# The attention output stored as two bf16 halves and loaded turned by transposing transfers

## The reference

```
x = x + xattn(layernorm(x), ctx, ctx, length)       # q, k with rope; softmax; 16 heads x 64
    out = softmax(q k^T / 8, masked) v              # [2048, 1024]
    return out @ Wo + bo                            # [2048, 256]
x = x + ffn(layernorm(x))                           # 8 experts, FF = 512, top 2 by a gate
```

## Time and profile before

| | before |
|---|---|
| runs, median (lowest to highest) | 1209.41 us (1206.67 to 1213.72) |
| span of the profiled execution | 1211.3 us |
| its mean granted clock of TensorE | 0.965 |
| PE, DVE, ACT, POOL busy | 1070.4, 979.4, 731.4, 644.6 us |
| last store issued, first load of the projection issued | 899.78, 906.04 us |
| first expert tile fetched | 1004.43 us |

### The profile page before, as it was taken

How to read it: one execution, slowest core, us unless ns; L and a number is a source line. 1 busy time by engine, 2 the same in 40 slices (tenths; PEclk the granted TensorE clock), 3 DMA queues, 4 the chain that set the end, 5 groups by cost and what they waited for, 6 DMA issues and landing times. The chain is left out here.

```text
span 1211.3 us, 32849 instructions
## 1 busy us (share of the span) xinstructions
PE 1070.4 (88%) x12843; PEld 709.2 (59%) x13030; DVE 979.4 (81%) x1769; ACT 731.4 (60%) x1298; POOL 644.6 (53%) x457
## 2 busy tenths in 40 slices
PE   1468999999999999999999999999969958999995
PEld 1334566566656656656665665666648944566663
DVE  5878999999999999999999999999944674455552
ACT  2635666666666666666666666766644643455552
POOL 1045764674585477467448647733449554333333
PEclk9679999999999999999999999999988979999998
DMA  8034242332423324143242433317526522333330
GB/s 280 0 97 115 79 107 63 98 91 69 107 79 97 96 81 104 51 122 84 77 99 76 110 79 90 79 38 224 207 99 231 174 84 84 57 52 57 54 60 12
DMA packets 104445, 117.01 MB, mean 97 GB/s; under 512 B 47389, under 2 KB 86494, under 8 KB 103006
## 3 DMA queue, kind: packets, MB, share of 16 engines
q1 hardware_dynamic: 91214, 99.74, 29.5%
q0 software_dynamic: 7152, 8.43, 4.2%
q10 hardware_dynamic: 5920, 6.65, 2.0%
HBM read 39.46 MB, written 36.87 MB: 63 GB/s over the span
## 5 line engine op out<-in xcount | busy, mean ns | idle before, releaser
L829 ACT ACTIVATE prob<-sc,key_bias 128x512 f32<-128x512 f32 x640 | 405.3, 684 | 149.2 <-PE sc L683 145.1
L962 DVE TENSOR_REDUCE part_max<-mx 128x1 f32<-128x427 f32 x768 | 417.3, 590 | 35.8 <-PE mx L700 35.8
L1106 POOL TENSOR_TENSOR prob_lo<-prob 128x1024 bf16<-128x1024 f32 x128 | 242.5, 1894 | 229.4 <-ACT prob L829 229.3
L974 DVE TENSOR_TENSOR prob_lo<-prob 128x1024 bf16<-128x1024 f32 x192 | 278.2, 1449 | 9.8 <-ACT prob L829 6.2
L727 PE MATMUL pv<-VV,prob 128*128 128x65 bf16 x2560 | 267.9, 193 | 3.7 <-POOL prob_lo L1106 3.5
L729 PE MATMUL pv<-VV,prob_lo 128*128 128x65 bf16 x2560 | 269.3, 195 | 0.0
L728 PE MATMUL pv<-VV,prob 128*128 128x64 bf16 x2560 | 268.0, 193 | 0.0
L727 PEld LDWEIGHTS pv<-VV,prob 128*128 128x128 bf16 x2560 | 239.8, 99 | 38.8 <-POOL prob_lo L1106 7.3
L728 PEld LDWEIGHTS pv<-VV,prob 128*128 128x128 bf16 x2560 | 237.2, 97 | 26.4
L683 PE MATMUL sc<-Q,K 65*128 65x512 bf16 x640 | 243.6, 381 | 10.3 <-issue 4.0
L700 PE MATMUL mx<-K,Q 128*128 128x427 bf16 x768 | 236.6, 349 | 9.7 <-DVE part_max L962 5.1
(11 more groups left out here) (208 smaller groups left out, 1470.8 us busy)
## 6 DMA issues: line engine op xcount, KB each, us to landing
expert_inputs<-zeros SPq DMA_DIRECT2D x129, 129.0 KB, 2.8
we<-in_w_exp SPq DMA_DIRECT2D x8, 1536.0 KB, 7.9
Q<-we SPq DMA_DIRECT2D x45, 256.0 KB, 3.8
attention_out<-o_out SPq DMA_DIRECT2D x64, 128.0 KB, 2.0
o_in<-attention_out SPq DMA_DIRECT2D x16, 512.0 KB, 3.7
q32s<-q SPq DMA_DIRECT2D x122, 64.0 KB, 2.0
K<-we SPq DMA_DIRECT2D x48, 160.0 KB, 3.9
VV<-next_v SPq DMA_DIRECT2D x16, 322.5 KB, 4.0
```

The costliest lines, as they stand in the source:

```text
L829: act.activation(prob[:, s % PRING, j, :], sc[n % 2][:], ACT.Exp, bias=key_bias[:, t:t + 1], scale=HD ** -0.5).then_inc(exp_done, 1)
L962: dve.tensor_reduce(part_max[:, b_ % 2, qt, h:h + 1], mx[:, pl.part_banks(qt, h)[0]:pl.part_banks(qt, h)[-1] + 1, 0:pl.width], mybir.AxisL ...
L974: dve.tensor_tensor(prob_lo[:, s % PRING, 0:g, :], prob[:, s % PRING, 0:g, :], hi_half(prob[:, s % PRING, 0:g, :])[:, :, 1::2], ALU.subtra ...
L1106: pool.tensor_tensor(prob_lo[:, s % PRING, 0:g, :], prob[:, s % PRING, 0:g, :], hi_half(prob[:, s % PRING, 0:g, :])[:, :, 1::2], ALU.subtr ...
```

## The change

The DRAM tensor `attention_out` becomes bf16 and twice as wide: for each head pair 128 columns of high halves and then 128 of low halves. `output` on POOL multiplies as before, then casts the result to bf16 (the high half) and subtracts that from the f32 value (the low half); each of the three instructions waits for the one before it by a semaphore. `store` waits for the low half and issues two DMAs of 64 KB in place of one of 128 KB. In the projection SP loads a tile, 128 rows x 2048 columns bf16, again 512 KB, with a transposing DMA into `oT`, where each run of 128 columns arrives turned. The transposes on PE and both splits, `OH` on ACT and `OL` on DVE, are gone, and the matmuls read `oT`. A buffer of `oT` is free when its projection has ended; a buffer of `o_in` was free when its transposes had ended.

```diff
-    o_dram = nc.dram_tensor("attention_out", [S, H * HD], F32, kind="Internal").ap()
+    o_dram = nc.dram_tensor("attention_out", [S, 2 * H * HD], BF16, kind="Internal").ap()
...
+        o_halves = sb("o_halves", [P, 2, 2, QT, HD], BF16)
...
                     def output(p, i):
 
                         need(pool, rden_made, p, BLOCKS, i + 1)
-                        need(pool, o_stored[i % 2], p, 16 * BLOCKS // 2, 16 * (i // 2 + 1))
+                        need(pool, o_stored[i % 2], p, 32 * BLOCKS // 2, 32 * (i // 2 + 1))
                         pool.tensor_tensor(o_out[:, i % 2, :, :], o_raw[:, i % 2, :, 0:HD], rden[:, i % 2, :].unsqueeze(2).to_broadcast([P, QT, HD]),
                                            ALU.mult).then_inc(o_made, 1)
+                        need(pool, o_made, p, BLOCKS, i + 1 + 2)
+                        pool.tensor_copy(o_halves[:, i % 2, 0, :, :], o_out[:, i % 2, :, :]).then_inc(o_hi_made, 1)
+                        need(pool, o_hi_made, p, BLOCKS, i + 1)
+                        pool.tensor_tensor(o_halves[:, i % 2, 1, :, :], o_out[:, i % 2, :, :], o_halves[:, i % 2, 0, :, :],
+                                           ALU.subtract).then_inc(o_lo_made, 1)
...
                     def store(p, i):
                         a, c = set_of(i)
-                        need(sp, o_made, p, BLOCKS, i + 1 + 2)
+                        need(sp, o_lo_made, p, BLOCKS, i + 1)
                         rows = o_dram[c * QC:(c + 1) * QC, :].rearrange("(t p) d -> p t d", p=P)
-                        sp.dma_start(rows[:, :, bass.ds(p * P + a * HD, HD)], o_out[:, i % 2, :, :]).then_inc(o_stored[i % 2], 16)
+                        for z in range(2):
+                            sp.dma_start(rows[:, :, bass.ds((2 * p + z) * P + a * HD, HD)], o_halves[:, i % 2, z, :, :]).then_inc(o_stored[i % 2], 16)
...
-        o_in = sb("o_in", [P, OB, J * P])
-        OH = sb("OH", [P, 2, J, P], BF16)
-        OL = sb("OL", [P, 2, J, P], BF16)
+        oT = sb("oT", [P, OB, 2 * J, P], BF16)
...
                 for t in range(ST):
                     if t >= OB:
-                        sp.wait_ge(ot_ready, t - OB + 1)
-                    sp.dma_start(o_in[:, t % OB, :], o_dram[t * P:(t + 1) * P, :]).then_inc(o_loaded[t % OB], 16)
+                        sp.wait_ge(wp_ready, t - OB + 1)
+                    sp.dma_start_transpose(oT[:, t % OB, :, :], o_dram[t * P:(t + 1) * P, :]).then_inc(o_loaded[t % OB], 16)
...
-                        act.wait_ge(ot_ready, t + 1)
-                        if t >= 2:
-                            act.wait_ge(wp_ready, t - 1)
-                        act.activation(OH[:, t % 2, :, :], ot[t % 2][:].rearrange("p b k c -> p (b k) c"), ACT.Copy).then_inc(oh_made, 1)
...
-                        dve.wait_ge(oh_made, t + 1)
-                        dve.tensor_tensor(OL[:, t % 2, :, :], ot[t % 2][:].rearrange("p b k c -> p (b k) c"), OH[:, t % 2, :, :],
-                                          ALU.subtract).then_inc(ol_made, 1)
...
-                        pe.wait_ge(o_loaded[t % OB], 16 * (t // OB + 1))
-                        if t >= 2:
-                            pe.wait_ge(ol_made, t - 1)
-                        for j in range(J):
-                            ins = pe.transpose(ot[t % 2][:, j // 4, j % 4, :], o_in[:, t % OB, j * P:(j + 1) * P], ident)
-                        ins.then_inc(ot_ready, 1)
                     t = step - 1
                     if 0 <= t < ST:
-                        pe.wait_ge(ol_made, t + 1)
+                        pe.wait_ge(o_loaded[t % OB], 16 * (t // OB + 1))
...
-                        steps = [(z, w, j) for j in range(J) for z, w in ((OH, wo_hi), (OH, wo_lo), (OL, wo_hi))]
+                        steps = [(z, w, j) for j in range(J) for z, w in ((0, wo_hi), (0, wo_lo), (1, wo_hi))]
                         pe.matmul(wp[t % 2][:, 0:D], ones_b[:], bias_rows[:], start=True, stop=False)
                         for n, (z, w, j) in enumerate(steps):
-                            ins = pe.matmul(wp[t % 2][:, 0:D], z[:, t % 2, j, :], w[:, j, :], start=False, stop=n == len(steps) - 1)
+                            ins = pe.matmul(wp[t % 2][:, 0:D], oT[:, t % OB, 2 * j + z, :], w[:, j, :], start=False, stop=n == len(steps) - 1)
```

More of the change, by code:

```diff
@@ L593, in attend @@
         seen = sem("seen")
-        o_made = sem("o_made")
+        o_made, o_hi_made, o_lo_made = sem("o_made"), sem("o_hi_made"), sem("o_lo_made")
         o_stored = [sem("o_stored0"), sem("o_stored1")]
@@ L1254, in program @@
                     for i in range(2):
-                        sp.sem_inc(o_stored[i], 16)
+                        sp.sem_inc(o_stored[i], 32)
                     def first_swap(m, halves):
@@ L1293, in program @@
                     for i in range(2):
-                        sp.wait_ge(o_stored[i], 16 + 16 * PAIRS * BLOCKS // 2)
+                        sp.wait_ge(o_stored[i], 32 + 32 * PAIRS * BLOCKS // 2)
                 for_key_count(sp, length, program)
@@ L1389, in project_and_mix @@
         ids_made, shift_made = sem("ids_made"), sem("shift2_made")
-        ot_ready, oh_made, ol_made = sem("ot_ready"), sem("oh_made"), sem("ol_made")
         wp_ready, x1_made, st_made, mv_made, sd_made, rs_made, nm_made = (sem(n) for n in (
@@ L1497, in _ @@
                 for step in range(STEPS):
-                    t = step
-                    if t < ST:
-                        act.wait_ge(ot_ready, t + 1)
-                        if t >= 2:
-                            act.wait_ge(wp_ready, t - 1)
-                        act.activation(OH[:, t % 2, :, :], ot[t % 2][:].rearrange("p b k c -> p (b k) c"), ACT.Copy).then_inc(oh_made, 1)
                     t = step - 2
```

## The result

| | before | after |
|---|---|---|
| runs, median (lowest to highest) | 1211.1 us (1206.7 to 1213.7), 4 runs | 1230.1 us (1229.7 to 1232.7), 4 runs |
| ratio after to before, 95% interval | | 1.0162 (1.0135 to 1.0189) |
| span of the profiled execution | 1211.3 us | 1227.8 us |
| from pair to pair in the attention (mean of 7) | 102.1 us | 105.0 us |
| start of the projection stage, S | 906.1 | 930.1 |

S is the first POOL instruction of the stage. A fourth run of the kernel before moved its median from 1209.4 to 1211.1. The change costs 1.6%. The spans differ by 16.5 us: the stage starts 24.0 later (20.8 of it by the start of the last pair, 3.2 at the end of the attention), gives 8.6 back until the first expert tile is fetched, and 1.2 goes in the rest. 1210 was forecast; 1230 lies inside the stated range of 1198 to 1243, and outside the likeliest case's own.

What follows compares the result with a forecast made beforehand. PE bounds plain attention blocks and the projection, DVE the heavy blocks with POOL close behind. Projection -16.5, attention +14 and its end +3 sum to +0.5 on 1211.3, so about 1210 us, range 1198 to 1243.

Steps and rivals of the forecast that it cites:

- likeliest case: Whole kernel: projection gain and attention loss cancel, about 1210 us, own range 1202 to 1218; rival 1, chance 0.36.
- rival 4: Projection stage: transposing loads can't keep up, PE waits at each tile; 1238 us at 5 us a load, 1287 at 8; chance 0.28.
- Attention, 2.0 a pair: Attention, seven head pairs: POOL's cast and subtraction delay heavy blocks, mainly the last, 2.0 us a pair, 14 us in all.
- bounds of 3 to 24: Attention loss in us: 3 if only part of the last heavy block shows, 24 if DVE's and POOL's slowdowns add up.
- Exclusion: POOL beside DVE's L974: contention not in full; by the full rule each new operation costs its whole length, the upper bound.
- Plain blocks, nothing: About 36 attention blocks without next-pair preparation: POOL's 2.17 us idle hides the two operations, no cost.
- End of the attention, +3.0: Last block to projection stage: output before it adds 1.3, cast and subtraction 1.3, second store issued 0.4 later; 3.0 us.
- Projection, -16.5: Projection stage: without PE transposes tiles take 3.18 us, last projection ends at S + 59.2; 16.5 us taken as gain.
- Can the tail follow?: After the projection: POOL's splits and scatters end not before S + 77.4, so the stage can give at most 18.9 us.
- The transposing load, hidden: Projection loads of 512 KB: priced near the plain load's 3.7 us, bounds 3.7 to 8, hidden behind the tiles.
- SP's queue, nothing: Attention stores: 64 more issues of 0.38 us; the swap behind has over 3 us of slack, so no cost.
- Rival 3: Attention: POOL and DVE saturate, 3.2 us a pair, 22 us in all, total 1218 us; chance 0.12.

Runs made afterwards that it cites:

- plain_load: Changed kernel with the 16 transposing loads replaced by plain ones, so the projection multiplies unturned data; fetch only 1.1 us earlier, total time not given.
- ops_only: Kernel before plus POOL's cast and subtraction only, halves unused, projection as before; ratio 1.016 to the kernel before.
- stage_only: Changed kernel whose POOL multiplication writes the bf16 high half directly, without cast or subtraction, low half zero, both stores kept; ratio 0.997 to the kernel before.
- cast_only: Changed kernel without POOL's subtraction, low half a zero set once, both stores kept; projection stage starts at 929.6 us, total time not given.
- batched_halves: Changed kernel with heavy blocks' outputs kept in float32 and halved later, two per plain block; those other five blocks sum to 62.8 us, before 59.4; total not given.
- high_only: Changed kernel without the low half (output rounded once to bf16), DVE doing 5 of 16 weight splits; ratio 0.992 to the kernel before, 1202 us.
- act_cast: Changed kernel with cast on ACT, subtraction and stores behind group 3's low, DVE doing 6 of 16 weight splits; stage starts at 950.2 us, total not given.

## Why the prediction was right and wrong

- *The number.* The highest chance (0.41) was on slower, but the likeliest case was a tie. The sum was +0.5; +16.5 was measured on the span. Of the 16 between them, 6.8 are the attention, 7.9 the stage, 0.2 the end of the attention and 1.2 the rest, all in the same direction. That 1230 lies in the range is luck: the range reached so high mostly for rival 4, the loads, which did not come.
- *Attention, 2.0 a pair.* 20.8 instead of 14; the bounds of 3 to 24 held. The length of the work was right, by errors that cancel: cast and subtraction were put at 0.3 and 0.55 us with two waits of 0.24; alone they take 0.40 and 0.67 with gaps of 0.06 to 0.08, 1.2 instead of 1.3, and 1.8 on average in company. The step that failed is how this reaches PE. It was to come late by POOL's `low`; that is 5.6 us, and 10.3 us are waits for DVE's partial maxima, behind DVE instructions that POOL's new ones hold up. For DVE's growth the sum had 0.2 a pair, 1.4 in all. By blocks (fifth pair): the last heavy output interval grew by 1.8 and the next gave 0.4 back (put at 1.3), and the second heavy one grew by 0.9, where "over 1 us of slack" was read. Adding up lengths can't find this, since the order in which instructions meet decides what a wait costs.
- *Exclusion.* I wrote that the trace agrees "not in full exclusion, as L1121 and L974 both grow". The earlier trace rows fit full exclusion too, to 0.14 us: DVE's `low` there began at 565.64 and ended at 567.22, 1.21 us (its length alone) after 566.01, about when POOL's `low` ended (566.15); L1121 began in the profile at 566.10 and ended at 567.69, 0.47 after DVE's, where 0.61 is its length. Both grew because each waited for the other in turn. The Trainium skill (SBUF — State Buffer, Who interferes with whom) states this, and that issue order decides who blocks; plain_load's five coincident ends agree. The sum worked out by that rule, the upper bound of 24, was nearer to 20.8 than my value.
- *Plain blocks, nothing.* Right: 10.9 to 11.0 in the last pair, with the cast there.
- *End of the attention, +3.0.* Right: the last output interval grew from 6.2 to 8.0, and from last multiplication to S it is 8.4 us instead of 7.0; +3.2.
- *Projection, -16.5.* The measured gain is 8.6, and 3.7 against a run with the same stage. The last projection ends at S + 68.8, not S + 59.2, term by term: first tile started at S + 7.7, not 4.5 (+3.2: the transposing load takes 7.7 us, near the upper of its two bounds); the slower first tile cost 2.7, put at 3 (-0.3); the tile is 3.31, not 3.18 (+1.4 over 11), since the 0.11 of gap did not go with the transposes; the stall is 7.8, not 3 (+4.8), 6.5 of it L1665 held by POOL's splits and 1.3 the slower clock behind it; 0.5 are small differences elsewhere. Before, this comparison began at 950.22, 0.46 us after the last split (949.76); the faster stage moved it forward by 8 us, into them. The same exclusion again, and the prediction asked only whether POOL could follow.
- *Can the tail follow?* POOL's scatters did not bind: the fetch follows the last projection by 20.9 us, before by 22.6.
- *The transposing load, hidden.* Right at 3.31 us a tile: PE never waits for one after the first. But the DMA engines, at 1.00 over 940 to 960, have little left. Worked out from the trace's packets, 2048 of 256 bytes per load at 21 ns on 16 engines are 2.7 us. Rival 4 was put to decide from 3.6 us on and did not come. The Trainium skill (Advanced Engine Details and Errata, X-Bar Transpose (TRN2)) has 350 to 400 GB/s; the stage moved 204 GB/s with all engines busy, and the measurement decides.
- *SP's queue, nothing.* Not separated from the second store; stores, queue and noise together are the 3.8 us between ops_only and the changed kernel, or the 1.6 of stage_only, which has both stores.
- *Rival 3* (POOL and DVE saturate, 22 us) had the attention's size right, at a chance of 0.12; its time was 1218, since it too had 16.5 from the stage.

Open: why the forms with an added POOL instruction, whose waits and clocks differ, all end at 104.6 to 105.5 us a pair, and what released DVE and ACT where the trace has no releaser.

## What to carry to other kernels

POOL's idle time beside a full DVE is not room: add up, for both engines together, the POOL work and DVE's instructions with two operands in SBUF, and see whether that still fits. A short instruction can take many times its length there (the comparison of 0.19 us took 7.49 behind POOL's splits). Of what was tried in the attention, neither moving nor shortening the added instructions was a remedy; leaving them out was. Before calling two equal losses one loss, compare what the bottleneck engine waits for in each, and the granted clock: the changed kernel, cast_only and batched_halves lose about the same 3 us a pair by three different waits. When work moves to an idle place, look for the instruction behind it that another engine waits for. When a change speeds up a stage, look at what fixed-length work of another engine the moved instructions now run into.

## What the runs showed of the hardware

- POOL instructions and DVE instructions with two SBUF operands exclude each other for whole instructions, and back-to-back POOL instructions may keep DVE out for several (7.49 us for 0.19) or give it one turn at each change (plain_load, cast_only, high_only). Which of the two it is, no run settles.
- Such a wait stands inside an instruction's duration, not in the idle before it; an engine that reads as busy may be blocked.
- After PE pauses of 1.84 us in cast_only the granted clock was at its lower level (0.50) for 3.4 us in six of seven cases; in the changed kernel, whose pauses there are at most 1.3 us, it stayed at the upper one.
- A transposing load of 512 KB as packets of 256 bytes: the first took 7.7 us from issue to landing, where the first plain one took 3.5, and all together 2.7 us (median) of SP's queue per issue, 204 GB/s at a DMA share of 1.00.
- In act_cast DVE and ACT stood still for 6.33 and 5.46 us and went on at the same moment, with no releaser known (DVE, then ACT):

```profile
1017.04 0.42 DVE L1765 TENSOR_TENSOR x<-wp,x 128x256 f32<-128x256 f32 x1 [6.33 <-remote]
...
1017.08 0.39 ACT L1533 ACTIVATE YF<-yt 128x256 f32<-128x256 f32 x1 [5.46 <-remote]
```
